# Routed experts of a perceiver layer: the hidden activations are transposed by VectorE and ScalarE in place of TensorE

## The reference, cut to what matters

```python
logits = xt @ W_router + routing_bias
probs = jax.nn.sigmoid(logits)
scores, idx = jax.lax.top_k(probs, TOPK)
scores = scores / jnp.sum(scores, axis=-1, keepdims=True)
g = jnp.einsum('th,ehi->tei', xt, Wg_r)
u = jnp.einsum('th,ehi->tei', xt, Wu_r)
hmid = silu(g) * u
combined = jnp.einsum('tei,eih,te->th', hmid, Wd_r, wts)
```

## Time and profile before

| | us |
|---|---|
| median of three runs | 812.97 |
| the profiled execution | 810.25 |
| its span | 808.4 |
| PE busy | 767.6 (95%) |
| DVE busy | 530.5 (66%) |
| ACT busy | 355.3 (44%) |
| POOL busy | 301.0 (37%) |
| routed tiles on PE, from the first matmul on tile 0 to the last D | 598.7 to 797.2 |

### The profile page before, as it was taken

One profiled execution on the slowest core, in us unless ns is written; L12 is line 12 of the kernel. 1 busy time (PEld: TensorE's weight loads), 2 busy tenths in 40 slices (PEclk: granted clock), 3 DMA queues, 4 the chain that ended last, 5 costly groups with the idle time before them and its releaser, 6 DMA issues.

```text
span 808.4 us, 17795 instructions
## 1 busy us (share of the span) xinstructions
PE 767.6 (95%) x6855; PEld 564.8 (70%) x6857; DVE 530.5 (66%) x1147; ACT 355.3 (44%) x913; POOL 301.0 (37%) x157
## 2 busy tenths in 40 slices
PE   4899999999899999999999999899999999997996
PEld 4554455554657778878877787677888888885884
DVE  5898797797644447676788888856475545544445
ACT  4356446562253428853258877723522122121221
POOL 1000000000431943643022222443639999994034
PEclk9999999999889999999999999999999999998999
DMA  9968666883511022040179000040658466531138
GB/s 342 386 254 304 209 245 233 318 318 125 223 33 74 0 60 101 2 127 12 52 270 384 25 0 1 2 157 2 228 179 296 135 209 200 184 111 45 52 116 274
DMA packets 56082, 127.08 MB, mean 157 GB/s; under 512 B 5057, under 2 KB 20673, under 8 KB 49873
## 3 DMA queue, kind: packets, MB, share of 16 engines
q1 hardware_dynamic: 36752, 105.44, 36.7%
q10 hardware_dynamic: 16704, 12.33, 4.8%
q0 software_dynamic: 2560, 8.39, 3.1%
HBM read 101.99 MB, written 24.15 MB: 156 GB/s over the span
## 4 chain that ended last, share of the span: by engine, by line
PE 61%; POOL 20%; DVE 8%; DMA 4%; ACT 3%; issue 3%; SPq 0%; POOLq 0%; DVEq 0%; ACTq 0%
PE scores L622 11%; PE bank L652 10%; POOL ring_lo L1365 10%; POOL ring_hi L1363 7%; DMA nat<-in_ctx_keys 3%; POOL picked L1378 2%; PE bank L702 2%; PE bank L856 2%; PE bank L703 2%; PE bank L857 2%; PE bank L862 2%; PE bank L704 2%; PE bank L1029 2%; PE bank L892 2%; PE bank L637 2%
## 5 line engine op out<-in xcount | busy, mean ns | idle before, releaser
L1845 DVE STREAM_TRANSPOSE ctxT<-nat 128x1024 f32<-128x1024 f32 (+3 forms) x124 | 116.8, 1003 | 8.5 <-DMA nat<-in_ctx_keys 8.2
L652 PE MATMUL bank<-nat,probT 128*64 128x512 f32 (+1 forms) x416 | 94.6, 601 | 0.1
L1365 POOL TENSOR_TENSOR ring_lo<-ring_raw,ring_hi 128x2048 fp32r<-128x2048 f32 x18 | 82.9, 4608 | 14.2 <-DVE ring_lo L2458 13.0
L1244 POOL TENSOR_TENSOR wq_lo<-wq_raw,wq_hi 128x1024 fp32r<-128x1024 f32 x4 | 9.3, 2357 | 210.4 <-ACT wq_hi L1476 210.4
L1150 PE MATMUL bank<-ring_hi,xg_lo 128*128 x180 | 72.7, 404 | 0.0
L1152 PE MATMUL bank<-ring_hi,xg_hi 128*128 x180 | 70.8, 393 | 0.0
L1151 PE MATMUL bank<-ring_lo,xg_hi 128*128 x180 | 70.6, 392 | 0.0
L652 PEld LDWEIGHTS bank<-nat,probT 128*64 128x64 f32 (+1 forms) x416 | 28.1, 137 | 52.0 <-issue 48.4
L2488 DVE TENSOR_TENSOR rhm_lo<-bank,rhm_hi 128x512 fp32r<-128x512 f32 x21 | 14.5, 692 | 73.0 <-ACT rhm_hi L1743 73.0
L622 PE MATMUL scores<-ctxT,hn 32*64 32x416 f32 (+8 forms) x1536 | 56.5, 427 | 5.1 <-issue 3.7
L622 PEld LDWEIGHTS scores<-ctxT,hn 32*64 32x64 f32 x1536 | 42.7, 131 | 21.3 <-issue 13.5
(11 more groups left out here) (316 smaller groups left out, 1914.7 us busy)
## 6 DMA issues: line engine op xcount, KB each, us to landing
nat<-in_ctx_keys SPq DMA_DIRECT2D x48, 1024.0 KB, 8.9
ring_raw<-in_Wexp SPq DMA_DIRECT2D x21, 1024.0 KB, 6.1
x_slots<-zeros SPq DMA_DIRECT2D x1, 5632.0 KB, 18.2
y_slots<-zeros SPq DMA_DIRECT2D x1, 5632.0 KB, 32.6
hn<-x_slots ACTq DMA_DIRECT2D x88, 64.0 KB, 2.1
y_slots<-hn ACTq DMA_DIRECT2D x22, 256.0 KB, 4.2
w_raw<-in_Wexp SPq DMA_DIRECT2D x3, 1024.0 KB, 5.6
nat<-in_ctx_keys SPq DMA_DIRECT2D x16, 130.0 KB
```

Of the source, the lines that this page charges most:

```text
L652: last = nc.tensor.matmul(context_bank(k)[64 * b:64 * b + 64, :], probT[0:n, j, 64 * b:64 * b + 64], nat[k % 2][0:n, b, j, :], start=j == ...
L1365: last = nc.gpsimd.tensor_tensor(ring_lo[at], ring_raw[at], ring_hi.bitcast(F32)[at], ALU.subtract)
L1845: dve.transpose(dst, src).then_inc(columns_ready, 1)
```

## The change

1. The activations of tiles 0 to 19 are transposed without TensorE. DVE transposes rhm in 32x32 blocks into a new buffer rhm_blocks (one instruction), and ACT moves the 16 block groups to their places in bank 3, one copy of 32 partitions x 128 elements for each pair of a source and a destination quarter of the partitions. DVE then rounds bank 3 (tensor_copy to rhm_hi) and subtracts (rhm_lo). Tiles 20 and 21 keep the PE transposes, and the PE order for the last tiles is T(20), gate of H(21), D(20), up of H(21), T(21), D(21).
2. T(0) to T(19) leave PE, so its order is H(t), D(t-1).
3. DVE copies the output of a tile out of PSUM (output_out); ACT only issues the store, after 13 of its 16 copies of the next tile.
4. The order on ACT for a tile is SiLU, row loads, spread; the loads are of the tile after the next but one (t+3). The rounding of the second expert's up matrix (second_high(1)) moves from ahead of tile 0's hidden_columns_out to behind SiLU of tile 1.
5. On DVE the order for a tile is value_load, routed_mult(t) with the block transpose, rows_columns(t+2) but for its last quarter of low parts, output_out(t-1), hidden_split(t), and that last quarter (rows_end), which now carries the wait for split_ready.
6. POOL rounds with tensor_scalar (add 0.0, one tensor read) in place of tensor_tensor with a broadcast zero.

```diff
+        rhm_blocks = place(156, "rhm_blocks", [P, HC, 4, B32])
+        rhmT = bank[3][:].rearrange("p (c q) -> p c q", q=P)
...
-            def routed_hidden(t, par, at):
-                if not (isinstance(t, int) and t < 2):
-                    hidden_columns(t - 1)
-                pe.wait_ge(xgT_ready, t + 1)
-                for m, b, full in ((gate, 1, rgate_full), (up, 2, rup_full)):
+            def routed_hidden(t, par, at, which=None):
+                which = which or (gate, up)
+                if gate in which:
+                    pe.wait_ge(xgT_ready, t + 1)
+                for m in which:
+                    b, full = (1, rgate_full) if m == gate else (2, rup_full)
                     if isinstance(t, int) and t == 0:
                         pe.wait_ge(down_added, NT - 2 if m == gate else NT - 1)
                     else:
                         pe.wait_ge(rsilu_ready if m == gate else rhm_ready, t)
                     routed_product(bank[b], m, at, xg_hi[par], xg_lo[par], full)
-                    if isinstance(t, int) and t == 1 and m == gate:
-                        hidden_columns(0)
-            def hidden_columns(t):
+            def last_hidden_columns(t):
                 pe.wait_ge(rhm_ready, t + 1)
-                if isinstance(t, int) and t == 0:
-                    pe.wait_ge(down_added, NT)
-                else:
-                    pe.wait_ge(rhmT_ready, t)
+                pe.wait_ge(rhmT_ready, t)
                 for c in range(HC):
                     last = nc.tensor.transpose(bank[3][:, c * P:(c + 1) * P], rhm[:, c * P:(c + 1) * P], ident)
-                last.then_inc(rhmT_full, 1)
+                last.then_inc(rhm_turned, 1)
...
-            routed_hidden(TILES - 1, 1, at[1])
-            hidden_columns(TILES - 1)
+            last_hidden_columns(TILES - 2)
+            routed_hidden(TILES - 1, 1, at[1], (gate,))
             routed_output(TILES - 2, 0, at[0])
+            routed_hidden(TILES - 1, 1, at[1], (up,))
+            last_hidden_columns(TILES - 1)
...
-                        nc.gpsimd.tensor_tensor(ring_hi[at], ring_raw[at], zero, ALU.add).then_inc(split_hi, 1)
+                        nc.gpsimd.tensor_scalar(ring_hi[at], ring_raw[at], 0.0, None, ALU.add).then_inc(split_hi, 1)
...
-            def hidden_columns_out(t):
-                act.wait_ge(rhmT_full, t + 1)
-                nc.scalar.copy(hidden_parts(t)[0][:].rearrange("p c q -> p (c q)"), bank[3][:]).then_inc(rhm_split, 1)
-            def output_rows(t, par, turn):
-                act.wait_ge(rdown_full, t + 1)
-                if not (isinstance(turn, int) and turn == 0):
-                    act.wait_ge(y_stored[par], 16 * turn)
-                nc.scalar.copy(yo[par][:], bank[4 + par][:]).then_inc(yo_ready, 1)
+            def hidden_columns_out(t, par):
+                act.wait_ge(rhm_turned, 2 * t if isinstance(t, int) and t == TILES - 1 else 2 * t + 1)
+                if isinstance(t, int) and t >= TILES - 2:
+                    last = nc.scalar.copy(hidden_parts(t)[0][:].rearrange("p c q -> p (c q)"), bank[3][:])
+                else:
+                    for g in range(4):
+                        for a in range(4):
+                            if (g, a) == (3, 1) and not (isinstance(t, int) and t == 0):
+                                output_rows(t - 1, 1 - par)
+                            last = nc.scalar.copy(rhmT[B32 * a:B32 * (a + 1), :, B32 * g:B32 * (g + 1)],
+                                                  rhm_blocks[B32 * g:B32 * (g + 1), :, a, :])
+                last.then_inc(rhm_split, 1)
...
-            second_high(1)
-            hidden_columns_out(0)
             act.wait_ge(xgT_full, 2)
             load_rows(3, 1)
-            routed_silu(1)
-            output_rows(0, 0, 0)
-            hidden_columns_out(1)
-            def routed_step(t, par, turn, load=True):
+            hidden_columns_out(0, 0)
+            def routed_step(t, par, load=True):
+                routed_silu(t)
+                if isinstance(t, int) and t == 1:
+                    second_high(1)
                 if load:
-                    act.wait_ge(xgT_full, t + 1)
-                    load_rows(t + 2, par)
-                routed_silu(t)
-                if isinstance(t, int) and t == TILES - 1:
-                    hidden_columns_out(t)
-                    output_rows(t - 1, 1 - par, turn)
-                else:
-                    output_rows(t - 1, 1 - par, turn)
-                    hidden_columns_out(t)
+                    act.wait_ge(xgT_full, t + 2)
+                    load_rows(t + 3, 1 - par)
+                hidden_columns_out(t, par)
+            routed_step(1, 1)
...
+            routed_step(TILES - 4, 0)
+            routed_step(TILES - 3, 1, load=False)
+            routed_step(TILES - 2, 0, load=False)
+            output_rows(TILES - 3, 1)
+            routed_silu(TILES - 1)
+            output_rows(TILES - 2, 0)
+            hidden_columns_out(TILES - 1, 1)
+            output_rows(TILES - 1, 1)
...
-                if not first:
-                    nth = dve.value_load(tile_expert[0:1, 1, ds(t, 1)], min_val=1, max_val=NR)
                 dve.wait_ge(xg_loaded[par], 64 * turn)
                 dve.transpose(xgT[par].rearrange("p a (g q) -> p a g q", q=B32),
                               xg[par].rearrange("p g (a e) -> p a g e", e=B32)).then_inc(xgT_full, 1)
@@ -2470,43 +2471,80 @@
                     last = dve.tensor_scalar(xg_hi[par][:, c, :], xgT[par][:, c, :], vec[:, V_W2B + c:V_W2B + c + 1], None, ALU.mult)
                 last.then_inc(xg_split, 1)
                 dve.wait_ge(xg_split, t + 1)
-                if not first:
+                for c in range(HC - 1):
+                    rows_low(par, c)
+            def rows_low(par, c):
+                return dve.scalar_tensor_tensor(xg_lo[par][:, c, :], xgT[par][:, c, :], vec[:, V_W2B + c:V_W2B + c + 1],
+                                                xg_hi[par].bitcast(F32)[:, c, :], ALU.mult, ALU.subtract)
+            def rows_end(par, nth=None):
+                if nth is not None:
                     dve.wait_ge(split_ready, nth)
-                for c in range(HC):
-                    last = dve.scalar_tensor_tensor(xg_lo[par][:, c, :], xgT[par][:, c, :], vec[:, V_W2B + c:V_W2B + c + 1],
-                                                    xg_hi[par].bitcast(F32)[:, c, :], ALU.mult, ALU.subtract)
-                last.then_inc(xgT_ready, 1)
+                rows_low(par, HC - 1).then_inc(xgT_ready, 1)
...
             def routed_mult(t):
                 dve.wait_ge(rup_full, t + 1)
                 dve.wait_ge(rsilu_ready, t + 1)
                 dve.tensor_tensor(rhm[:], rhm[:], bank[2][:], ALU.mult).then_inc(rhm_ready, 1)
+                if not (isinstance(t, int) and t >= TILES - 2):
+                    dve.wait_ge(rhm_ready, t + 1)
+                    dve.transpose(rhm_blocks[:].rearrange("p c a q -> p (c a q)"), rhm[:]).then_inc(rhm_turned, 1)
             def hidden_split(t):
                 dve.wait_ge(rhm_split, t + 1)
-                hi, lo = hidden_parts(t)
-                dve.tensor_tensor(lo[:].rearrange("p c q -> p (c q)"), bank[3][:],
-                                  hi.bitcast(F32)[:].rearrange("p c q -> p (c q)"), ALU.subtract).then_inc(rhmT_ready, 1)
+                if isinstance(t, int) and t >= TILES - 2:
+                    hi, lo = hidden_parts(t)
+                    dve.tensor_tensor(lo[:].rearrange("p c q -> p (c q)"), bank[3][:],
+                                      hi.bitcast(F32)[:].rearrange("p c q -> p (c q)"), ALU.subtract).then_inc(rhmT_ready, 1)
+                    return
+                if not (isinstance(t, int) and t == 0):
+                    dve.wait_ge(rdown_full, t)
+                dve.tensor_copy(rhm_hi[:], rhmT).then_inc(rhm_turned, 1)
+                dve.wait_ge(rhm_turned, 2 * t + 2)
+                dve.tensor_tensor(rhm_lo[:], rhmT, rhm_hi.bitcast(F32)[:], ALU.subtract).then_inc(rhmT_ready, 1)
...
+            def output_out(t, par, turn):
+                dve.wait_ge(rdown_full, t + 1)
+                if not (isinstance(turn, int) and turn == 0):
+                    dve.wait_ge(y_stored[par], 16 * turn)
+                dve.tensor_copy(yo[par][:], bank[4 + par][:]).then_inc(yo_ready, 1)
+            def hidden_and_next(t, par, turn):
+                nth = need_of(t + 2)
+                routed_mult(t)
+                rows_columns(t + 2, par, turn + 1)
+                if not (isinstance(t, int) and t == 0):
+                    output_out(t - 1, 1 - par, turn - 2 + par)
+                hidden_split(t)
+                rows_end(par, nth)
+            for t in range(4):
+                hidden_and_next(t, t % 2, t // 2 + 1)
+            with dve.Fori(0, TILES // 2 - 3) as i:
                 for par in range(2):
-                    t = 2 * i + 1 + par
-                    rows_columns(t + 1, par, i + 2)
```

(31 more changed lines are left out.)

13 lines of the change are left out of this document (3 added, 10 removed).

## The result

The changed kernel takes 852.38 us (median of 4 runs, 850.27 to 855.25); the kernel before took 812.82 beside it. The ratio is 1.0485, with a 95% interval from 1.044 to 1.053: 39.6 us slower, where 9.8 faster was forecast. The profiled execution took 852.13, its span 850.1.

What follows compares the result with a forecast made beforehand. POOL's matrix splitting was taken to bound until 737.6, then PE. The schedule gained 10.1 (pieces: 9.3 transposes, 5.4 PE idle, 1.7 clock, less 2.6, 2.4, 1.8); less 0.3 tail, 9.8 gave 803.2 us, range 798.5 to 816.5.

Steps and rivals of the forecast that it cites:

- the rounding on POOL: POOL's rounding of each expert matrix: 1.9 us in place of 3.605, taken by the memset's 1.81; break-even at 2.70.
- Case A: Rival, chance 0.18: POOL still sets the pace; with rounding at 3.6 the gathers start 3.3 later, 816.3 us.
- the end: Stretch from the first gather to the end of the span: 28.7 us before, with 0.3 taken for the change.
- the later store: Store of tile 18, the last used tile: 2.6 behind its down product in place of 0.8, costing 1.8 us.
- Removing the transposes: On PE, tiles 0 to 18: 0.49 us saved each, 9.3 for 19, leaving PE's own limit at 8.16 a tile.
- the loop on DVE: DVE's cycle from one tile's multiplication to the next: about 8.3 us, expected to set the period, 0.14 above PE.
- The copies: ACT's 16 copies a tile from SBUF into PSUM: 0.305 us each, 4.9 together, hidden behind PE's work.
- case B: Rival, chance 0.14: the loop through ACT and DVE binds, period 8.7 to 8.9, gain 0 to 3, 811.5 us.
- The stand ahead of D(0): At the start, PE idles once for 2.6 us before tile 0's down product, awaiting the new chain.
- second_high(1) delayed POOL: ACT's moved rounding of the second expert's up matrix ends near 613.3, so POOL's third low part starts 3.9 us late.
- POOL's chain as the bound of the kernel before: POOL's splitting of the expert matrices holds the kernel from 600 to 737.6; PE sets the pace only after it.
- the rigid distance from the ring to the end of the tiles: After POOL's last expert matrix is split, PE's tiles follow until the last used tile's store at 776.73.

Runs made afterwards that it cites:

- the kernel with the slow rounding and the old end: Changed kernel, tensor_scalar on POOL kept, with only the order of its last tiles put back to that of the kernel before: 841.48 us, ratio 1.0368.
- The run without gathers: Changed kernel with POOL rounding by adding zeros, and POOL's first gather waiting for the last tile's down product: 830.91 us in a single run.
- the pair with the same end: Changed kernel and kernel before, both with tensor_copy and PE's sums over gathered rows ahead of tile 21's transposes: 810.42 and 812.94 us.

## Why the prediction was wrong

**The step that failed** is the one that took the rounding on POOL as 1.9 ("If writes go beside them, one read hides under the write"). It bounded an operation that no row showed by the memset below and the two-tensor operation above, on the ground that "one read should not be above two". The instruction takes 5.375, outside both ends, in the old schedule and in the new one. The number of tensors read does not rank these operations on POOL: the copy and the scalar form both read one, and the scalar form takes 2.8 times as long. Case A of the prediction held the mechanism and its slope (816.3 at 3.6, "each 0.1 adds 1.5"); at 5.375 it gives 842.9, and the kernel with the slow rounding and the old end took 841.5. Its chance of 0.18, and the range's upper end at 816.5, came from the false bound.

**The second term that was mis-sized is the end**, given 0.3 on top of 28.7, beside 1.8 for the later store. It measured 42.6, and the new order costs 12 of it (42.5 to 43.3 against 31.0). The prediction saw the series and put the last output copy at 787, 17.4 behind its first gather (769.6), at the speed that PE and DVE have without gathers. The run without gathers bears that speed out: there the copy is 18.8 behind tile 20's multiplication, with gathers 30.4; and that multiplication comes 0.5 behind the first gather in the changed kernel. Neither the forecast nor its rivals had a term for PE's late semaphores; the profile of before showed none.

**Point by point.** Removing the transposes was priced at 0.49 a tile. It brought 0.2: PE's period was 8.65 and is 8.16 and 8.71 in turn. The price of the transposes held, as the 8.16 shows. The 0.55 in every second tile is new. The first matmul of H(19), where PE's loop turns:

```profile
794.00 0.49 PE L1152 MATMUL bank<-ring_hi,xg_lo 128*128 x1 [0.25 <-issue]
```

In the kernel before PE did not stand there: the first matmuls of two tiles in a row, one of them behind a turn, look alike and are 8.64 apart.

```profile
708.34 0.48 PE L1150 MATMUL bank<-ring_hi,xg_lo 128*128 x1
716.98 0.48 PE L1150 MATMUL bank<-ring_hi,xg_lo 128*128 x1
```

With the transposes ahead of it the turn cost nothing that the records show; without them it takes back half of what they gave, a term that the prediction left out. The period of 8.43 stands against 8.3 forecast, and its maker is PE, not the loop on DVE. The copies (0.27 against 0.305) made that loop 7.8 in place of 8.3, so case B never arose, though the store's issue did fall into the spread as it feared. The stand ahead of D(0) is 1.9 (2.6 forecast). second_high(1) delayed POOL by 1.1, not 3.9: it began at 608.42 in the changed kernel, where the prediction has it near 611.4. Of these 3 us, 2.3 are luck, as the tiles began that much sooner in this profile.

**What held**: POOL's chain as the bound of the kernel before, the rigid distance from the ring to the end of the tiles, and case A for a rounding of 3.6 (816.3 forecast, 814.2 measured with the old end; 826.0 with the end that case A priced). With tensor_copy and the old end the kernel takes 801.3 and 802.9; the forecast was 803.2. That is luck in part. The period and the end (31.0 against 29.0) are both longer than forecast; against them stand the shorter stand ahead of D(0), tiles that began 3.4 and 1.1 sooner in the two profiles than in that of before, and a median only 0.9 and 0.1 above the profiled execution, where 2.7 was taken. And most of the gain is the rounding: the kernel before with tensor_copy alone is at 0.9913. What the turning and the spread add to that is small: 0.9891 and 0.9896 against it, with intervals that overlap, and the 2.5 us of the pair with the same end.

**Open**: why PE's semaphores are late beside the gathers, and by how much. The stretch from the multiplication of tile 20 to that of 21 was 22.2 to 22.4 in all kernels with PE's new order and gathers beside it. With the old order it was 8.6 and 10.1 in the kernel before, 11.7 to 11.8 in the changed one, and 16.3 and 17.7 in the kernel before with another rounding (tensor_copy alone gave 17.7 in one profile and 16.3 in the next). A transfer of instructions falls into the wait in the four profiles of the changed kernel with the old end (at about 777 in the fastest); in the changed kernel itself the only one of the end comes at about 834, behind both waits, so it is not the common cause. That the new order is late only with gathers rests on one run without them; the mechanism is not shown. Which of PE's or DVE's order does it was separated only as far as the additions: a kernel with PE's order alone put back wasn't tried, as the output copy of tile 20 must move with it.

## What to carry to other kernels

Where an edit rests on an operation that no row shows, on an engine that is waited for, measure it, or let the range reach past every neighbour; on POOL round by a plain copy, not by adding a scalar zero. In the stretch where gathers run, let PE make first what another engine waits for: with D(20) ahead of tile 21's up product, and DVE's output copy with it, the multiplication came 10.5 later here than with both behind it. Put the work that needs no other engine ahead of such a wait, but do not count the wait as saved: it hid 3.5 to 4 us of additions and the late product came no sooner.

## What the runs showed of the hardware

POOL, 128x2048 from f32 to the rounded type: tensor_copy 1.900 us, tensor_tensor with a broadcast column 3.605, tensor_scalar 5.375; memset of the shape 1.814. The Trainium skill (GPSIMD Engine Reference, Engine selection) calls one-input work there roughly line-rate. The copy agrees, at 1.900 against 2.28 for VectorE's subtraction of two tensors of the shape, and the scalar form does not.

ACT, 32 partitions: copies of 32x128 from SBUF into PSUM follow each other after 0.27 us, against 0.625 for 32x512.

PE's semaphores under gathers: from the end of the last recorded matmul to DVE's use, the down product of tile 20 took under 0.1 us without and 5.1 with them, the up product of tile 21 under 0.1 and 10.9. In other orders of work the up product's was 0 to 9.1 with gathers.

PE: a turn of the loop of 72 matmuls without transposes at its head cost about 0.55 us (periods 8.71 and 8.16); with them no gap shows.
